# New instruction orders in a sparse attention, longer tile lists for two expert layers, and chains at stage ends spread over engines

## The chip, the cores and the metric

The kernel runs on one core of a Trainium2 chip. The metric is the device time of one execution in microseconds (us).

## The reference

A block of four layers with residuals over x of 16 x 256 tokens with 128 channels, all float32. `norm` is a layer norm.

```python
x = x + linear_attention(norm(x))     # 4 heads; softmax over k's tokens; its own norm and residual inside
x = x + ffn(norm(x))
x = x + sparse_attention(norm(x))
x = x + ffn(norm(x))                  # the same weights

def ffn(x):                           # 8 experts, 128 -> 512 -> 128
    probs = softmax(x @ Wr + br)
    e, gate = argmax(probs), max(probs)
    return (relu(x @ W1[e] + b1[e]) @ W2[e] + b2[e]) * gate

def sparse_attention(x):              # each of 256 queries of a batch keeps 32 keys
    Q, K, V = split(x @ w_qkv.T + b_qkv); Q, K = rope(Q), rope(K)
    iq, ik, iw = ...                  # 4 index heads of 64, one weight for each head
    scores = sum_h relu(iq[h] @ ik.T) * iw[h]
    bias = 0 at the 32 largest scores of a row, -inf elsewhere
    return softmax(Q @ K.T / sqrt(128) + bias) @ V @ w_o.T + b_o
```

## The kernel before

Tokens lie in 32 tiles of 128 (two tiles make one batch, `b`). Each engine has its own list of instructions, written out by hand; they meet in semaphores. The stages follow each other:

1. **Linear attention** (`steps` over 16 batches, a software pipeline: `st.item(k)` is the batch that entered k steps ago). Its end turns the normalised rows (`turn_xf` on TensorE, `xf_out` on ScalarE), multiplies by the router (`router`) and copies the logits (`logits_out`), batch by batch, in `bank[6]`.
2. **Routing 0.** `route_differences`, `route_exp`, `route_choices` and `route_gates` are done for tiles 0 to 23 (k = 0) and 24 to 31 (k = 1). Then ranks, the places of all tokens in the order by expert (`is_tile`, `oneh_slot`, and 32 matmuls at L600), the lists `te` (expert) and `ti` (tile) of the 39 pieces of work and the gather indices `gidx`. `keep_clock` on TensorE issues transposes whose result nobody reads.
3. **Experts 0.** GpSimd gathers sorted rows from DRAM (L427). Step s on TensorE: turn tile s (L620), first layer of piece s-1 (L629), second layer of piece s-2 (L639). ScalarE copies the turned tile (L836) and the expert's first weights (L841) and makes half of `hT` (L849), VectorE the other half (L1184), then `gm` (L1176), `yb` (L1190) and the sum into `big` (L1196). The entries of `te` and `ti` are read into registers by `loaded` (L297), eight at a time, on TensorE, ScalarE and VectorE. TensorE moves on when both halves of `hT` are there.
4. **Sparse attention.** Rows come back by a gather of `X` (L447, `gather_x`). One step s works on several batches at once: projections, index scores and head sums of batch s, the selection of the 32 largest of batch s-1 (four rounds of MAX8, L1335, and MATCH_REPLACE8, L1338), softmax and PV of batch s-2, the next router's rows of batch s-3. VectorE's list of a step is:

```python
mask_logits(0); add_third(b, r, 1); add_fourth(0); mask_logits(1); add_fourth(1)
for i in range(4):
    MAX8 and MATCH_REPLACE8 for both halves
    # i == 0: xf_b (L1267), shifts (nb, L1242)
    # i == 2: attended (L1250, L1255), spread_x2 (L1215)
    # i == 3: add_third(next, r, 0) (L1279), spread_x3 (L1222), aggregate_both (mv, L1234)
```

GpSimd's list of a step is: cosine product (L481), sine product (L483), their sum `qr` (L487), `add_heads` for both halves (`head_sum`, L466), `inverse_std` (`vpe`, L458, and the power `rs`, L460), `X + bo` (L493), and two gathers (L447). The third-head addition needs `head_sum`, `inverse_std` needs `mv`, `nb` needs `rs`, and ScalarE's next `xb` (L866) needs `nb`. ScalarE copies the index weights `iw` from PSUM (L922); their bias comes by a matmul with one row (L713).

5. **Routing 1** and **experts 1**: as 2 and 3, with a scatter of each finished tile to the output (L433) among the gathers of GpSimd: at step s it issues gather s+8 and then scatter s-8.

The functions that the change touches:

## Time and profile before

| | us |
|---|---|
| median of 3 runs | 523.01 (522.72 to 523.64) |
| the profiled execution | 523.16 |
| its span, first to last instruction | 521.3 |
| busy TensorE, VectorE, ScalarE, GpSimd | 437.5, 377.2, 337.8, 290.4 |
| a step of the sparse attention | 11.40 |
| from a piece to the next in the expert stages | 1.90 |

Linear attention takes the first 84 us, routing 0 up to 110, experts 0 up to 193, the sparse attention up to about 405, routing 1 up to 428, experts 1 to the end. No engine is busy all the time, and each stage has another limit, so the shares of the whole span say little: the page is read by stage, with the timeline of one step, and at each idle stretch with the instruction that ended it (in brackets behind `<-`). "issue" is time in which an engine waited for nothing that the profile shows. The granted clock of TensorE is given as a share of 2.4 GHz, so 0.50 is 1.2 GHz.

### The profile page before, as it was taken

The page shows a single profiled execution, that of the slowest core. Times are in us where ns is not written, and L with a number is a line of the kernel's source. Part 1 is how long each engine was busy: PE and PEld are TensorE (multiplying, and loading weights), DVE is VectorE, ACT ScalarE, POOL GpSimd, SP SyncE. Part 2 cuts the span into 40 slices and gives each one's busy share as a digit, 9 for nine tenths or more (in the row PEclk, how much of TensorE's full clock was granted, in tenths as well). Part 3 has the DMA queues.
Part 4 walks back from the last instruction along what each step waited for, and adds up shares of the span by engine and source line. Part 5 has one row for each costly group of instructions (what it writes and reads, how often), then busy time and mean ns, then how long its engine had stood idle before and what let it go on. Part 6 is the DMA issues. An engine that isn't in the chain of part 4 may idle for free. (4 is left out here: it accounts for less than half of the span.)

```text
span 521.3 us, 11629 instructions
## 1 busy us (share of the span) xinstructions
PE 437.5 (84%) x3048; PEld 383.1 (73%) x3048; DVE 377.2 (72%) x1501; ACT 337.8 (65%) x934; POOL 290.4 (56%) x329
## 2 busy tenths in 40 slices
PE   2689995799999896999988999998876599999981
PEld 1579894788988885667767777776655599988981
DVE  4789984836666651389999999999997656666661
...
GB/s 228 289 163 79 65 82 82 1 73 110 110 90 43 34 37 32 4 17 32 31 31 32 32 45 48 31 32 31 21 21 42 22 27 107 78 77 79 67 42 20
DMA packets 45070, 32.42 MB, mean 62 GB/s; under 512 B 13524, under 2 KB 39508, under 8 KB 45012
## 3 DMA queue, kind: packets, MB, share of 16 engines
...
## 5 line engine op out<-in xcount | busy, mean ns | idle before, releaser
L427 POOL DMA_INDIRECT big<-rows,gidx x64 | 61.6, 963 | 56.7 <-DVE gidx L1152 28.3
L639 PE MATMUL bank<-WE,hT 128*128 x624 | 83.6, 277 | 7.5 <-ACT hT L849 6.0
L629 PE MATMUL bank<-X,w 128*128 x624 | 83.4, 277 | 1.2 <-ACT X L836 0.4
L639 PEld LDWEIGHTS bank<-WE,hT 128*128 128x128 f32 x624 | 75.9, 192 | 9.6 <-issue 9.5
L629 PEld LDWEIGHTS bank<-X,w 128*128 128x128 f32 x624 | 75.8, 192 | 3.2 <-issue 3.1
L668 PE MATMUL bank<-xbT,WB 128*128 128x256 f32 x224 | 60.2, 400 | 9.3 <-ACT iq L890 8.7
L1184 DVE TENSOR_SCALAR hT<-bank,w 128x128 f32<-128x128 f32 x156 | 47.5, 346 | 22.7 <-PE bank L629 11.3
L841 ACT ACTIVATE w<-WE 128x644 f32 x78 | 57.2, 734 | 3.9 <-DVE big L1196 3.4
L447 POOL DMA_INDIRECT X<-x,pidx x32 | 31.7, 990 | 47.4 <-DMA x<-big 39.9
L836 ACT ACTIVATE X<-bank 128x128 f32<-128x128 f32 x64 | 17.8, 278 | 59.1 <-PE bank L620 58.9
L668 PEld LDWEIGHTS bank<-xbT,WB 128*128 128x128 f32 x224 | 40.1, 195 | 20.3 <-ACT iq L890 14.8
L849 ACT ACTIVATE hT<-bank,w 128x128 f32<-128x128 f32 x156 | 48.4, 365 | 9.5 <-PE bank L629 9.5
L1338 DVE MATCH_REPLACE8 wk<-m,wk 128x256 f32<-128x256 f32 x128 | 51.2, 407 | 0.0
L1335 DVE MAX8 m<-wk 128x8 f32<-128x256 f32 x128 | 47.4, 411 | 0.0
L433 POOL DMA_INDIRECT out<-big,gidx x32 | 31.4, 982 | 15.7 <-DVE big L1196 9.6
L687 PE MATMUL bank<-ik,iq 64*128 64x256 f32 x256 | 39.0, 403 | 0.8 <-ACT big L932 0.7
L1196 DVE SCALAR_TENSOR_TENSOR big<-yb,gm,big 128x128 f32 x78 | 27.6, 354 | 16.0 <-DVE yb L1190 14.2
L932 ACT ACTIVATE big<-bank 128x512 f32<-128x512 f32 x64 | 34.7, 596 | 2.5 <-PE bank L687 1.5
L1190 DVE TENSOR_TENSOR yb<-bank,w 128x128 f32<-128x128 f32 x78 | 22.6, 290 | 13.7 <-PE bank L639 13.3
L1279 DVE SCALAR_TENSOR_TENSOR wk<-big,iw,head_sum 128x256 f32<-128x256 f32 x32 | 21.1, 660 | 14.8 <-POOL head_sum L466 14.8
L937 ACT ACTIVATE big<-big,iw 128x256 f32<-128x256 f32 x64 | 29.0, 500 | 1.0
L514 PE MATMUL bank<-cst 128*128 128x128 f32 x188 | 28.4, 325 | 0.9 <-DVE big L1196 0.9
...
## 6 DMA issues: line engine op xcount, KB each, us to landing
...
big<-rows,gidx POOLq DMA_INDIRECT x64, 2.8
...
```

The source lines that it names most:

```text
L427: pool.indirect_dma_start(xg[:, j, :], None, rows_dram[n], bass.IndirectOffsetOnAxis(ap=gidx[:, j:j + 1], axis=0)).then_inc(f["g"][j % G_R ...
L447: pool.indirect_dma_start(X[:, t, :], None, x2_dram, bass.IndirectOffsetOnAxis(ap=pidx[:, t:t + 1], axis=0)).then_inc(b_["x"][r], 16)
L629: mm = pe.matmul(bank[r + 2 * (k // 2)][:, k % 2 * P:(k % 2 + 1) * P], w1[st.slot(1, 4)][:, k * P:(k + 1) * P], moving, start=True, stop=True)
L639: mm = pe.matmul(bank[4 + r][:, 0:D], hT[r][:, k, :], WE[:, bass.ds(expert[(s - 2) % TURN], 1), W2_AT + k * D:W2_AT + (k + 1) * D].rearran ...
L668: mm = pe.matmul(to, WB[:, i * D:(i + 1) * D], xbT[r][:, :], start=True, stop=True)
L687: mm = pe.matmul(bank[h % 2][:, h // 2 * S:(h // 2 + 1) * S], iq[r][lo:lo + IDX_DIM, h // 2, c * P:(c + 1) * P], ik[r][lo:lo + IDX_DIM, :] ...
L841: act.activation(w1[st.slot(0, 4)][:, :], WE[:, bass.ds(expert[st.base], 1), 0:W1_LEN].rearrange("p a w -> p (a w)"), ACT.Copy).then_inc(f ...
L849: act.activation(hT[r][:, k, :], bank[r][:, k * P:(k + 1) * P], ACT.Relu, bias=w1[st.slot(1, 4)][:, B1_AT + k:B1_AT + k + 1]).then_inc(f[" ...
L932: act.activation(rel[r][:, c, i::2, :], bank[i][:, :].rearrange("p (h k) -> p h k", h=2), ACT.Relu).then_inc(b_["rel"], 1)
L1184: dve.tensor_scalar(hT[r][:, k, :], bank[2 + r][:, k % 2 * P:(k % 2 + 1) * P], w1[st.slot(1, 4)][:, B1_AT + k:B1_AT + k + 1], 0.0, ALU.add ...
L1335: dve.max(m8[:, c, :], wk[r][:, c, :]).then_inc(b_["v"], 1)
L1338: dve.match_replace(wk[r][:, c, :], m8[:, c, :], wk[r][:, c, :], NEG).then_inc(b_["v"], 1)
```

## The change

- **Sparse attention, VectorE:** both masks first, then both third and both fourth additions, all at the head of a step; the first third addition no longer stands at the end of the step before. `index_weights`, the addition of the index bias, is a VectorE instruction after the second round; the copy on ScalarE and the matmul with one row go away. `nb` of batch 0 is made before the statistics of batch 1.
- **Sparse attention, GpSimd:** the first head sum goes ahead of `qr`, and the gathers ahead of `X + bo`.
- **TensorE there:** the turn of the probabilities of the first half goes behind the last projection.
- **Tile lists:** ScalarE and VectorE load 32 entries at once, then the remaining 7; TensorE loads 32 tiles and 20 experts before its first step, 19 experts at step 22 and 7 tiles at step 33.
- **Ends of stages:** the last three batches of the first stage turn in two banks alternately, with the turn of one ahead of the router of the one before. `route_differences`, `route_exp`, `route_choices` and `route_gates` of the first 24 tiles move to other places in both stages' ends. The number of `keep_clock` transposes changes, and there are new ones.

```diff
+LIST, EXPERTS = 32, 20
...
-KEEP_ROUTE, KEEP_GATHER = 32, 60
+KEEP_SLOTS, KEEP_ROUTE, KEEP_RANK, KEEP_GATHER, KEEP_STATS = 22, 28, 8, 44, 14
...
+        def late(b):
+
+            return bank[2] if isinstance(b, int) and b >= B - 3 and b % 2 else bank[6]
...
-            for c in range(C):
-                sp.dma_start(rowc[:, c * IDX_HEADS:(c + 1) * IDX_HEADS], b_iw).then_inc(ld_w, 16)
+            sp.dma_start(biw_bc[:, :], b_iw.rearrange("a e -> (a e)").partition_broadcast(P)).then_inc(ld_w, 16)
...
                                        ALU.mult).then_inc(b_["rp"], 1)
+                    add_heads(b, r, 0)
                     pool.wait_ge(b_["rp"], 2 * (b + 1))
                     after(pool, b_["S"], C * (b - 1))
                     pool.tensor_tensor(qr[r][:, :, :], qk[r][:, 0:2, :], qk[r][:, 2:4, :], ALU.add).then_inc(b_["qr"], 1)
-                    add_heads(b, r, 0)
                     add_heads(b, r, 1)
                 inverse_std(s)
+                if b + 3 < B:
+                    gather_x(b + 3)
                 if b < B:
                     pool.wait_ge(b_["xb"], b + 1)
                     pool.tensor_tensor(X[:, b * C:(b + 1) * C, :], X[:, b * C:(b + 1) * C, :],
                                        bo_bc[:, :].unsqueeze(1).to_broadcast([P, C, D]), ALU.add).then_inc(b_["xo"], 1)
-                if b + 3 < B:
-                    gather_x(b + 3)
...
-            def turn_xf(n, b, r, where):
+            def turn_xf(n, b, r, where, spare=0):
...
-                after(pe, t["xfT"], b)
-                after(pe, t["lg"], b)
+                after(pe, t["xfT"], b - spare)
+                after(pe, t["lg"], b - spare)
...
                 if st.base == 6:
-                    pe.wait_ge(ld_w, 80)
+                    pe.wait_ge(ld_w, 64)
+                if st.base >= B + 2:
+                    if st.on(5, B):
+                        keep_clock(3, bank[1][:, 0:P])
+                        turn_xf(0, st.item(5), st.slot(5, 2), late(st.item(5)), 1)
                 if st.on(6, B):
-                    router(0, st.item(6), st.slot(6, 2), bank[6][:, S:S + C * E])
+                    router(0, st.item(6), st.slot(6, 2), late(st.item(6))[:, S:S + C * E],
+                           int(st.base >= B + 4))
...
-                if st.on(5, B):
+                if st.on(5, B) and st.base < B + 2:
...
+                keep_clock(KEEP_RANK, bank[1][:, 0:P])
                 pe.wait_ge(rt["rank"], n + 1)
...
-                keep_clock(KEEP_ROUTE, bank[2][:, 0:P])
+                keep_clock(KEEP_SLOTS, bank[2][:, 0:P])
...
-                    if s % TURN == 1 and st.on(1, NT):
-                        tile = loaded(mybir.EngineType.PE, ti, s - 1, TURN, T - 1)
-                    if s % TURN == 2 and st.on(2, NT):
-                        expert = loaded(mybir.EngineType.PE, te, s - 2, TURN, E - 1)
+                    if s == 0:
+                        tile = loaded(mybir.EngineType.PE, ti, 0, LIST, T - 1)
+                        expert = loaded(mybir.EngineType.PE, te, 0, EXPERTS, E - 1)
+                    if s - 1 == LIST:
+                        tile = loaded(mybir.EngineType.PE, ti, LIST, NT - LIST, T - 1)
+                    if s - 2 == EXPERTS:
+                        expert = loaded(mybir.EngineType.PE, te, EXPERTS, NT - EXPERTS, E - 1)
...
-                        moving = xgT[:, bass.ds(tile[(s - 1) % TURN], 1), :].rearrange("p a d -> p (a d)")
+                        moving = xgT[:, bass.ds(tile[(s - 1) % LIST], 1), :].rearrange("p a d -> p (a d)")
...
-                                           WE[:, bass.ds(expert[(s - 2) % TURN], 1), W2_AT + k * D:W2_AT + (k + 1) * D
+                                           WE[:, bass.ds(expert[(s - 2) % EXPERTS], 1), W2_AT + k * D:W2_AT + (k + 1) * D
...
             keep_clock(KEEP_GATHER, bank[4][:, 0:P])
+            pe.wait_ge(b_["x"][0], 16 * C)
+            keep_clock(KEEP_STATS, bank[4][:, 0:P])
...
+                if st.base == B + 1:
+                    keep_clock(10, bank[2][:, 0:P])
...
                     b, r = st.item(2), st.slot(2, 2)
                     after(pe, b_["prT"], b)
-                    turn_probabilities(b, r, 0)
                 if st.on(0, B):
                     project(3)
                 if st.on(2, B):
+                    turn_probabilities(b, r, 0)
                     turn_probabilities(b, r, 1).then_inc(b_["PT"], 1)
...
-                    pe.matmul(bank[5][:, S:S + C * IDX_HEADS], ones[0:1, :], rowc[:, 0:C * IDX_HEADS], start=True, stop=False)
...
-                                       WB[:, 9 * D:9 * D + IDX_HEADS], start=False, stop=(c == C - 1))
+                                       WB[:, 9 * D:9 * D + IDX_HEADS], start=True, stop=True)
...
+                if st.base == B + 1:
+                    keep_clock(2, bank[2][:, 0:P])
...
+                if st.base == B + 2:
+                    keep_clock(8, bank[2][:, 0:P])
...
+                if st.on(5, B) and st.base >= B + 2:
+                    xf_out(0, st.item(5), st.slot(5, 2), late(st.item(5))[:, 0:S])
                 if st.on(6, B):
-                    logits_out(0, st.item(6), bank[6][:, S:S + C * E])
+                    logits_out(0, st.item(6), late(st.item(6))[:, S:S + C * E])
+                if st.base == B + 2:
+                    route_exp(0, 0)
...
-                if st.on(5, B):
+                if st.on(5, B) and st.base < B + 2:
...
-                    if opens(st, 0) and st.on(0, NT):
-                        expert = {}
-                        count = HEAD if st.base == 0 else NT - T if st.base == T else TURN
-                        for k, v in enumerate(loaded(mybir.EngineType.Activation, te, s, count, E - 1)):
-                            expert[st.base + k] = v
+                    if s % LIST == 0 and st.on(0, NT):
+                        expert = loaded(mybir.EngineType.Activation, te, s, min(LIST, NT - s), E - 1)
...
-            route_exp(0, 0)
...
+                if st.base == B + 1:
+                    route_exp(1, 0)
...
-                if st.on(0, B):
-                    act.wait_ge(b_["pj"], 5 * (b + 1))
-                    after(act, b_["wk"], C * (b - 1))
-                    act.activation(iw[r][:, :, :],
-                                   bank[5][:, S:S + C * IDX_HEADS].rearrange("p (c h) -> p c h", c=C),
-                                   ACT.Copy).then_inc(b_["iwe"], 1)
                 for c in range(C):
...
                             after(act, b_["hs"], C * (b - 1))
-                            act.wait_ge(b_["iwe"], b + 1)
                         for i in range(2):
...
                         act.wait_ge(b_["rel"], 2 * (C * b + c + 1))
+                        act.wait_ge(b_["iwe"], b + 1)
                         for h in range(2):
...
-                if st.base == B + 1:
-                    route_exp(1, 0)
...
+                if st.base == B + 1:
+                    dve.wait_ge(ld_wb, 48)
+                    dve.wait_ge(rt["exp0"], 1)
+                    route_differences(0, 0)
...
-                    if opens(st, 2) and st.on(2, NT):
-                        tile = {}
-                        count = HEAD - 2 if st.base == 2 else 9 if st.base == T else TURN
-                        for k, val in enumerate(loaded(mybir.EngineType.DVE, ti, s - 2, count, T - 1)):
-                            tile[st.base - 2 + k] = val
+                    if (s - 2) % LIST == 0 and st.on(2, NT):
+                        tile = loaded(mybir.EngineType.DVE, ti, s - 2, min(LIST, NT - (s - 2)), T - 1)
...
-                        at = bass.ds(tile[st.base - 2], 1)
+                        at = bass.ds(tile[(s - 2) % LIST], 1)
...
-            dve.wait_ge(ld_wb, 48)
-            dve.wait_ge(rt["exp0"], 1)
-            route_differences(0, 0)
...
+
+            def index_weights(b, r):
+
+                dve.wait_ge(b_["pj"], 5 * (b + 1))
+                dve.tensor_tensor(iw[r][:, :, :], bank[5][:, S:S + C * IDX_HEADS].rearrange("p (c h) -> p c h", c=C),
+                                  biw_bc[:, :].unsqueeze(1).to_broadcast([P, C, IDX_HEADS]), ALU.add).then_inc(b_["iwe"], 1)
...
-            shifts(Step(0), 0)
+                if u == -2:
+                    shifts(Step(0), 0)
...
-                if st.on(1, B):
-                    b, r = st.item(1), st.slot(1, 2)
                 if st.on(2, B):
                     p, q = st.item(2), st.slot(2, 2)
                     mask_logits(0)
+                    mask_logits(1)
                 if st.on(1, B):
+                    b, r = st.item(1), st.slot(1, 2)
+                    after(dve, b_["pen"], C * (b - 1))
+                    add_third(b, r, 0)
                     add_third(b, r, 1)
                     add_fourth(0)
-                if st.on(2, B):
-                    mask_logits(1)
-                if st.on(1, B):
                     add_fourth(1)

                 def beside(i):

+                    if i == 1 and st.on(0, B):
+                        index_weights(st.item(0), st.slot(0, 2))
                     if i == 0 and st.on(3, B):
                         xf_b(st)
+                    if i == 0 and st.base == B + 1:
+                        route_differences(1, 0)
                     if i == 0 and st.on(-1, B):
                         shifts(st, -1)
...
-                    if i == 3 and st.on(0, B):
-                        after(dve, b_["pen"], C * (st.item(0) - 1))
-                        add_third(st.item(0), st.slot(0, 2), 0)
...
-                if st.base == B:
-                    route_differences(1, 0)
                 if st.base == B + 1:
                     route_choices(1, 0)
+                if st.base == B + 2:
                     route_gates(1, 0)
```

## Rows read from the trace of the kernel before

**Rows 1.** Busy time of three stretches (stretch, us, busy and count by engine, clock, DMA)
```profile
206.00:208.00 2.00, 2.00 (x6) 1.61 (x5) 0.28 (x2) 0.84 (x2) 0.00 (x0) 0.51 0.00 0
284.58:295.98 11.40, 10.45 (x66) 8.24 (x65) 10.95 (x47) 10.62 (x30) 9.49 (x10) 1.00 0.14 35
448.80:497.00 48.20, 45.15 (x392) 43.89 (x391) 29.79 (x113) 33.12 (x93) 36.90 (x38) 1.00 0.25 73
```

**Rows 2.** Timeline of VectorE over the turn of a step (start us, us, what)
```profile
305.56 0.92 DVE L1279 SCALAR_TENSOR_TENSOR wk<-big,iw,head_sum 128x256 f32<-128x256 f32 x1 [0.28 <-POOL head_sum L466]
306.40 0.48 DVE L1222 BATCH_NORM_STATS2 stat<-X 128x6 f32<-128x128 f32 x2
...
308.02 0.48 DVE L1285 SCALAR_TENSOR_TENSOR wk<-big,iw,wk 128x256 f32<-128x256 f32 x1
...
310.60 0.59 DVE L1267 TENSOR_SCALAR xf<-X,mv,rs 128x128 f32<-128x128 f32 x2
311.11 0.15 DVE L1242 SCALAR_TENSOR_TENSOR nb<-mv,rs 128x2 f32<-128x2 f32 x1
```

**Rows 3.** Timeline of GpSimd in the same step
```profile
307.47 0.20 POOL L458 TENSOR_TENSOR vpe<-mv,eps 128x4 f32<-128x4 f32 x1 [1.27 <-DVE mv L1234]
307.75 1.26 POOL L460 TENSOR_TENSOR rs<-vpe,mhalf 128x4 f32<-128x4 f32 x1
309.00 0.82 POOL L493 TENSOR_TENSOR X<-X,bo_bc 128x256 f32<-128x256 f32 x1
309.99 1.04 POOL L447 DMA_INDIRECT X<-x,pidx  x1 [0.17 <-issue]
311.33 0.95 POOL L447 DMA_INDIRECT X<-x,pidx  x1 [0.30 <-issue]
```

**Rows 4.** Timeline of VectorE and GpSimd at 368 us
```profile
367.99 1.54 DVE L1267 TENSOR_SCALAR xf<-X,mv,rs 128x128 f32<-128x128 f32 x2
...
368.10 1.34 POOL L481 TENSOR_TENSOR big<-big,cst 128x512 f32<-128x512 f32 x1 [0.89 <-ACT big L890]
...
369.45 1.24 DVE L1242 SCALAR_TENSOR_TENSOR nb<-mv,rs 128x2 f32<-128x2 f32 x1
```

**Rows 5.** The line of the first power (durations min/median/max, start, forms)
```profile
L382 POOL TENSOR_TENSOR r<-v,mhalf x5: 1045/2900/2911, 7.2 to 31.9; 128x16 f32<-128x16 f32 x3, 128x4 f32<-128x4 f32 x1, 128x12 f32<-128x12 f32 x1
```

**Rows 6.** Timeline of TensorE at two of the eight holes
```profile
126.20 1.06 PE L629 MATMUL bank<-X,w 128*128 x8
...
129.56 1.15 PE L629 MATMUL bank<-X,w 128*128 x8
...
494.70 1.06 PE L629 MATMUL bank<-X,w 128*128 x8
...
498.52 1.15 PE L629 MATMUL bank<-X,w 128*128 x8 [0.23 <-DVE hT L1184]
```

**Rows 7.** The line that loads registers (ns min/median/max, first and last start)
```profile
L297 ACTq TENSOR_LOAD <-te x10: 543/548/985, 103.9 to 491.9; - x10
L297 PEldq TENSOR_LOAD <-ti x10: 587/594/778, 109.7 to 493.5; - x10
L297 DVEq TENSOR_LOAD <-ti x10: 810/1870/2306, 112.9 to 493.6; - x10
```

**Rows 8.** Timeline at the end of the first stage
```profile
89.16 0.18 ACT L758 ACTIVATE logits<-bank 128x16 f32<-128x16 f32 x1 [1.11 <-PE bank L508]
...
91.88 0.16 DVE L1035 TENSOR_TENSOR r_a<-logits,br_bc 128x64 f32<-128x64 f32 x1
```

**Rows 9.** Timeline at the start of the sparse attention
```profile
203.17 0.88 ACT L866 ACTIVATE xb<-X,nb,rs 128x128 f32<-128x128 f32 x2 [11.39 <-DVE nb L1242]
```

**Rows 10.** Timelines of VectorE and TensorE at the second routing
```profile
398.49 0.42 DVE L1293 CUSTOM_DVE_ANT_0 lg<-bank,pen 128x256 f32<-128x256 f32 x1
...
420.02 4.11 PE L600 MATMUL bank<-oneh_tile,oneh_slot 128*128 128x64 bf16 x32
```

**Rows 11.** Timeline of the last scatter
```profile
511.94 0.97 POOL L433 DMA_INDIRECT out<-big,gidx  x1 [0.30 <-DVE big L1196]
```

18 lines of the change are left out of this document (9 added, 9 removed).

## Prediction

> **What bounds the kernel now.** I read the page first, then the profile by stage. In the middle of the sparse attention one step (one batch of 256 tokens) takes 11.40 us, VectorE is busy 10.95 of it, ScalarE 10.62, TensorE 10.45, and each of the other engines could do with less [rows 1]. So the question is who waits for whom. The timeline of VectorE shows it: at 305.56 the first third-head addition (L1279) starts late, behind GpSimd's `head_sum`, and then takes 0.92 us, where its twin L1285 takes 0.48 [rows 2]. GpSimd in turn waits for `mv` before it starts the inverse deviation [rows 3]. That is a ring: aggregate, GpSimd's whole list of a step, head sum, addition, statistics, aggregate. The wait before the addition is 0.35 us and the addition holds VectorE 0.84 us (305.56 to 306.40), so L1279 at this place costs 1.19 us a step.
>
> Why 0.92? GpSimd ran the second head sum. The clearest case is at 368: `xf` takes 1.54 us for two tiles (0.59 otherwise) and `nb` 1.24 us (0.15 otherwise), each until GpSimd's tensor-tensor of that moment ends (L481 from 368.10 to 369.44, then L483) [rows 2, 4]. VectorE instructions with two SBUF inputs, and `xf`, thus wait for a GpSimd tensor-tensor that began before them. Whoever is first wins, and the order of both lists decides it.
>
> The expert stages are bound by TensorE at 1.90 us a tile, except once every eight tiles: from 126.20 to 129.56 is 3.36 us, and from 494.70 to 498.52 it is 3.82 [rows 6]. There are eight such holes; together they take 13.0 us more than normal tiles (1.90, and 1.79 where no row is turned any more). What they share is the load of the next list entries into registers: 0.55 us on ScalarE, 0.59 on TensorE, but a median of 1.87 on VectorE [rows 7], and TensorE then waits for `hT`. The ends of the stages (clock 0.5, engines mostly waiting) are serial chains.
>
> **Ends of the first stage, routing 0.** Before, the last logits land at 89.34, and only then come the exponential, `choices` and `gates` of the first 24 tiles; the second part begins at 91.88, 2.54 us later [rows 8]. In the new order these are done while TensorE still works on the last batches, so the second part follows the logits directly: -2.5. The turns of the last three batches now overlap in two banks: the last logits come some 1.1 us earlier at the low clock (the three extra transposes a step eat part of it). `KEEP_SLOTS` of 22 lets the slot matmuls start when the slots are ready, about 0.4 earlier here. Together -4.0, bounds -2.5 (no overlap won) and -5.5 (full clock).
>
> **Experts 0.** The four holes vanish: -6.6 of the 13.0. What comes back: VectorE loads 7 entries at step 34 (1.0 taken, between 0.2 and 1.7), TensorE reloads 19 experts and 7 tiles (0.5 together), and at the start TensorE loads 32 + 20 entries in front of its first transpose. The cost of a long load is not in the trace. Bounds: the time doesn't depend on the count (eight entries 0.55, seven 0.985 on ScalarE, so it is not proportional [rows 7]), or it grows with the count: 52 x 0.59/8 = 3.8 us on TensorE, 32 x 1.87/8 = 7.5 us on VectorE. I take about 1.2 us for 32 and 1.0 for 20, one small step for each further eight. Before, the first loads were partly hidden behind the keep-clock transposes and gathers; I charge 0.7. VectorE's first load of 32 stands at step 2, where the second `hT` has some 1 us of slack: free at 1.5 us, dear at 7.5. Sum -6.6 + 1.5 + 0.7 = -4.4.
>
> The Trainium skill speaks against this part: "Runtime: NRT & Kernel Launch", Instruction fetch mechanics, gives about 200 ns a register for such a load even in bulk. By it eight registers would take 1.6 us, and the row for ScalarE says 0.55, so the trace does not agree. By the page's figure, as an estimate, 52 registers would hold TensorE 10.4 us in each expert stage, and the sum would end near 522.
>
> **Start of the sparse attention.** `nb` of batch 0 stood behind the statistics of batch 1, which waited for their gather; ScalarE idled 11.39 us until 203.17 [rows 9]. Now it follows the inverse deviation, at 201.8: -1.2. TensorE gets 14 more transposes after the first gather, so its gap shrinks from 4.0 to 1.6 us; the granted clock, 0.51 from 206 to 208 [rows 1], may hold: I take -0.8 of a possible -1.7. Sum -2.0.
>
> **A step of the sparse attention.** Time zero is the end of the aggregate (307.39). VectorE before: first mask at -0.08, `xf` at 3.21, `nb` at 3.72 [rows 2]. The change puts both masks first, then both thirds and both fourths: one more addition ahead, so `xf` goes to 3.61, its second tile to 3.86, `nb` to 4.12. Taken out of the end of the step: 1.19. Added: 0.40 for the addition without wait, 0.17 for `index_weights` (an addition of 128x8 from PSUM). Step: 11.40 - 1.19 + 0.57 = 10.78.
>
> Now GpSimd. Before: `vpe` at 0.08, power at 0.36 for 1.26, `X + bo` at 1.61, gathers at 2.60 and 3.94 [rows 3]. The power alone takes 1.05 (the 128x4 form of L382 [rows 5]); the 0.21 more is L1279 at 0.23. In the new order a mask stands there, from PSUM, and doesn't block: power ends at 1.41. Then the gathers: the first starts into a fourth (1.37 to about 1.72), then 1.03 + 0.31 + 0.95, ending at 4.01. So `X + bo` asks at about 4.03, in the middle of the second tile of `xf` (3.86 to 4.04) and before `nb` (4.12). It wins against `nb`, which waits until 4.75: +0.50. The step becomes 11.28, 0.12 less than before; 12 steps give -1.4. Without that clash 10.78, -7.4. This is the finest reading of the whole sum: 0.2 us either way changes its sign.
>
> ScalarE loses L922 and the 0.53 us before the second exponential; it could do 10.5. TensorE loses L713. Neither sets the step. The wait for `iwe` now falls on VectorE's second round (5.8), when TensorE wants to turn `xf` (5.5 to 5.8); queued behind it are the scores of the second half and S, with over 0.5 us of slack: nothing.
>
> **The rest.** `route_differences(1, 0)` stood before the last masks (at 398.49, 0.95 late [rows 10]) and now hides in the 3.4 us wait for PV: -0.95. The last `xf` no longer waits for `gates`: -0.6. The slot matmuls began at 420.02, because 32 transposes at half clock were ahead, with the slots ready at 418.8: -1.25 [rows 10]. Gathers start 2.8 earlier. In experts 1 GpSimd is as full as TensorE: from 448.80 to 497.00 it issues 38 gathers and scatters, 36.9 us busy plus 0.30 between two [rows 1]. Without holes TensorE would gain 6.4 less 1.5, but it has the long loads in front, and then the scatters, issued 1.28 apart, set the end. Following that list, the first scatter comes 1.9 earlier, 15 pairs later it is still packed, and the last scatter (511.94 [rows 11]) falls at about 506.9: -5.0 for all of this paragraph.
>
> **Sum.** -4.0 - 4.4 - 2.0 - 1.4 - 5.0 = -16.8. The profiled execution took 523.16 us (span 521.3), the median of the runs is 523.01; so 523.0 - 16.8 = 506.2. I say 506. Its own range is 501 to 511.
>
> **Rivals.**
> 1. *No clash of `nb`* (20%). If `X + bo` asks 0.2 us later, `nb` passes and a step is 10.78: 506 - 6 = 500. For it: rows of single instructions jitter by 0.02 only, but the sum of five durations is not that sure.
> 2. *A double clash* (18%). If `X + bo` asks before 3.95, it beats the second tile of `xf`, and then the cosine product beats `nb`, as at 368 [rows 4]. `nb` ends at 5.87: a step of 12.4, +13 instead of -1.4: 520. Against it: 0.08 us.
> 3. *Long loads are dear* (12%). With the proportional cost TensorE loses 1.6 and VectorE some 4 more in each stage: 506 + 11 = 517.
> 4. *Slower than before* (5%). VectorE's load: six entries took 0.81, eight 1.87 [rows 7], a slope of 0.53 an entry. If that holds, 32 entries take 14.6 us in front of the second `hT`, and every engine stands: +12.6 in each stage, 506 + 25 = 531. It decides from a load of about 10 us on; below that the kernel is still faster.
> 5. *GpSimd's power blocks too*. The Trainium skill, "SBUF — State Buffer", SBUF: two separate sides, says that whoever starts first holds the pair for the whole instruction. The power from 0.36 to 1.41 would then hold up the third at 0.57 for 0.84 us a step, 10 us in all, 516. Rows speak against it: L1285 ran at 0.63 (308.02) in 0.48 us inside a power of 1.26 [rows 2, 3], so I give it 3%.
> 6. *The change does nothing measurable* (2%): gains in the stages given back in the sparse attention, 523.
>
> My forecast has the remaining 40%. From 498 to 521 leaves out no more than 2 in 10: below it only a case in which clock and clash both turn out well, above it dear loads or two bad cases at once. Faster by more than 0.2% (about what a measurement of this kernel can tell): 0.92; within: 0.02; slower: 0.06.
>
> **What would show it.** A step between aggregates of 11.3 us, with `nb` (the shift before the second round) at 0.7 instead of 0.15 us; 0.15 says rival 1, 1.7 with a long `xf` says rival 2. No wait of VectorE for `head_sum`. Third additions at 0.48. No hole at every eighth tile, one each near step 22 and 34. The duration of the register load with 32 entries: about 1.2 to 1.5 us is my case, above 4 rival 3. The second part of routing 0 starts right behind the last logits. Scatters packed until the end. I am wrong if loads of 32 take long, or if `X + bo` arrives elsewhere than at 4.0.

## The result, and the profile after

The changed kernel takes 530.24 us (median of 10 runs, 528.25 to 533.32), the kernel before, beside it, 522.77 us: a ratio of 1.013, 95% interval 1.0104 to 1.0157. It is slower by a little over 1%. (Ratios here and below are the recorded ones; the quotient of two medians differs from them by up to 0.002.) The prediction was 506 us, with 498 to 521 as range and 6% for slower. One of the four executions of run 10 below, the profiled one, fell in a slower state of the chip (547.88 us), so its time and ratio go by the other three, and of its trace only the steps of the sparse attention are read.

The profiled execution of the changed kernel took 528.76 us, its span is 526.9 (521.3 before), and the mean granted clock of TensorE is 0.916 (0.938 before). First, where the time went, by landmarks that both kernels have: the indices of the gathers (`gidx`), the first gather of `X` in the sparse attention, the first MAX8, the last aggregate, and the last scatter.

| stretch | before | after | difference | in the sum |
|---|---|---|---|---|
| start to `gidx` of routing 0 | 105.39 | 98.51 | -6.9 | -4.0 |
| to the first gather of `X` (experts 0) | 90.61 | 87.24 | -3.4 | -4.4 |
| to the first MAX8 (start of the sparse attention) | 22.77 | 19.51 | -3.3 | -2.0 |
| to the last aggregate (sparse attention) | 186.20 | 208.75 | +22.6 | -1.4, and its tail some -1.5 |
| to `gidx` of routing 1 | 19.45 | 17.86 | -1.6 | with experts 1 some -3.5 |
| to the last scatter (experts 1) | 87.52 | 85.66 | -1.9 | (see above) |
| to the end | 9.37 | 9.37 | 0 | 0 |

So every stretch around the sparse attention gained, 17.0 us together, and the sparse attention lost 22.6. The lines with the first and last starts of these landmarks, of the kernel after (the three numbers after the count are ns, minimum, median and maximum):

```profile
L1170 DVE CAST gidx<-idxf x2: 181/182/183, 98.5 to 431.9; 128x32 uint32<-128x32 f32 x2
L451 POOL DMA_INDIRECT X<-x,pidx x32: 938/959/1183, 185.8 to 362.0; - x32
L1354 DVE MAX8 m<-wk x128: 401/409/424, 205.3 to 405.6; 128x8 f32<-128x256 f32 x128
L1246 DVE BATCH_NORM_AGGREGATE mv<-stat x64: 146/150/183, 190.1 to 414.0; 128x2 f32<-128x6 f32 x64
L1285 DVE TENSOR_SCALAR xf<-X,mv,rs x32: 332/633/3191, 226.4 to 415.7; 128x128 f32<-128x128 f32 x32
```

The last line is the find. `xf` took 10.3 us in all before (32 tiles of 0.34 us median, one of them 1.29); now it is 37.2 us, a median of 0.63 and up to 3.19 for one tile. Busy time of two steps of the kernel after, measured between the ends of two aggregates (columns as in [rows 1]), stands against the one step of 11.40 there:

```profile
289.26:304.08 14.82, 11.80 (x60) 8.72 (x58) 13.82 (x48) 10.90 (x31) 9.13 (x10) 0.80 0.10 28
304.08:316.72 12.64, 12.60 (x68) 10.35 (x69) 11.47 (x48) 9.96 (x28) 9.20 (x10) 0.83 0.11 31
```

From the third batch's aggregate on the steps, taken between the starts of the aggregates, are 12.98, 10.82, 13.79, 13.81, 11.82, 14.45, 12.63, 14.82, 12.64, 14.82, 13.81, 12.61, 14.82 us. The one of 10.82 is the last in which VectorE has no `xf` to do yet; the trouble starts with the first `xf`. VectorE in the step of 14.82 us (start us, us, what), the answer to [rows 2]:

```profile
293.87 3.74 DVE L1285 TENSOR_SCALAR xf<-X,mv,rs 128x128 f32<-128x128 f32 x2
297.53 0.15 DVE L1254 SCALAR_TENSOR_TENSOR nb<-mv,rs 128x2 f32<-128x2 f32 x1
```

And GpSimd beside it, the answer to [rows 3]:

```profile
293.33 0.96 POOL L451 DMA_INDIRECT X<-x,pidx  x1 [0.30 <-issue]
294.32 0.76 POOL L499 TENSOR_TENSOR X<-X,bo_bc 128x256 f32<-128x256 f32 x1
295.05 1.26 POOL L485 TENSOR_TENSOR big<-big,cst 128x512 f32<-128x512 f32 x1
296.27 1.25 POOL L487 TENSOR_TENSOR big<-big,cst 128x512 f32<-128x512 f32 x1
```

The reader is to see that `xf` ends when the sine product ends (297.52): its second tile got nothing while `X + bo`, the cosine product (L485) and the sine product (L487) ran one behind the other. `nb` was never held, it was only late. The two tiles by themselves:

```profile
L1285 DVE TENSOR_SCALAR xf<-X,mv,rs x2: 630/1910/3191, 293.9 to 294.4; 128x128 f32<-128x128 f32 x2
```

The first took 0.63 us where 0.33 is usual, and so the second, which starts 0.25 us after the first where nothing is in the way, started at 294.42, 0.10 after `X + bo` (294.32). In the shorter steps (xf at 308.22, 1.29 us for two tiles) the cosine product had to wait for ScalarE, and only `X + bo` came between.

What follows from the late `nb`, on ScalarE and TensorE in the same step:

```profile
297.72 0.88 ACT L886 ACTIVATE xb<-X,nb,rs 128x128 f32<-128x128 f32 x2 [2.91 <-DVE nb L1254]
```
```profile
298.65 0.69 PE L671 MATMUL bank<-cst,xb 128*128 128x128 f32 x2 [2.48 <-ACT xb L886]
```

TensorE stands for 2.5 us in such a step, and its granted clock in three stretches of 25 us is 0.86, 0.84 and 0.80 (1.00 before in the stretches beside them), so part of the next step runs at the lower of the two levels (1.2 instead of 2.4 GHz; 341.00 to 343.00 shows 0.50):

```profile
230.00:255.00 25.00, 20.02 (x98) 15.54 (x99) 24.69 (x95) 18.77 (x50) 15.93 (x19) 0.86 0.11 30
280.00:305.00 25.00, 21.98 (x119) 17.11 (x119) 22.84 (x88) 20.02 (x54) 16.19 (x18) 0.84 0.12 33
330.00:355.00 25.00, 21.31 (x108) 16.47 (x106) 23.70 (x89) 17.94 (x50) 16.45 (x18) 0.80 0.12 32
```

The loads of the tile lists, whose price the prediction had to guess (beside [rows 7]): four on each engine and list, two of the full 32 (TensorE's experts 20) and two of the rest.

```profile
L302 DVEq TENSOR_LOAD <-ti x4: 1065/1596/2364, 106.8 to 504.5; - x4
L302 ACTq TENSOR_LOAD <-te x4: 974/1482/2159, 97.3 to 498.7; - x4
L302 PEldq TENSOR_LOAD <-ti x4: 1070/1634/2322, 100.2 to 500.4; - x4
L302 PEldq TENSOR_LOAD <-te x4: 1362/1612/1925, 102.5 to 477.3; - x4
```

### The profile page after: what moved, and what is told of

Its sections match the earlier page's. It is cut to its first block, busy times and chain, and to the rows that moved or that the text cites. A ratio compares the mean times of both kernels' runs of the same rounds, so it can differ in the third digit from the quotient of the medians.

```text
span 526.9 us, 11585 instructions
## 1 busy us (share of the span) xinstructions
PE 443.9 (84%) x3031; PEld 388.9 (74%) x3031; DVE 401.1 (76%) x1517; ACT 333.5 (63%) x918; POOL 286.3 (54%) x329
## 4 chain that ended last, share of the span: by engine, by line
PE 39%; DVE 19%; issue 14%; POOL 9%; ACT 9%; DMA 1%; POOLq 0%; ACTq 0%; DVEq 0%; SPq 0%
PE bank L642 12%; PE bank L652 12%; DVE xf L1285 5%; PE bank L683 3%; DVE wk L1357 3%; DVE m L1354 3%; PE bank L518 2%; ACT big L947 2%; PE bank L702 2%; PE bank L610 2%; DVE wk L1304 2%; PE bank L761 2%; PE bank L633 1%; DVE wk L1298 1%; POOL X L451 1%
## 5 line engine op out<-in xcount | busy, mean ns | idle before, releaser
L683 PE MATMUL bank<-xbT,WB 128*128 128x256 f32 x224 | 63.9, 432 | 7.2 <-ACT iq L910 6.4
L683 PEld LDWEIGHTS bank<-xbT,WB 128*128 128x128 f32 x224 | 45.7, 216 | 20.6 <-ACT iq L910 11.3
L470 POOL TENSOR_TENSOR head_sum<-big 128x256 f32<-128x256 f32 x32 | 23.3, 727 | 41.6 <-ACT big L953 41.6
L702 PE MATMUL bank<-ik,iq 64*128 64x256 f32 x256 | 41.1, 431 | 0.1
L1211 DVE SCALAR_TENSOR_TENSOR big<-yb,gm,big 128x128 f32 x78 | 27.6, 354 | 16.0 <-DVE yb L1205 15.4
L1285 DVE TENSOR_SCALAR xf<-X,mv,rs 128x128 f32<-128x128 f32 x32 | 37.2, 1202 | 0.5 <-POOL rs L464 0.5
L886 ACT ACTIVATE xb<-X,nb,rs 128x128 f32<-128x128 f32 x32 | 14.2, 500 | 34.1 <-DVE nb L1254 34.0
L518 PE MATMUL bank<-cst 128*128 128x128 f32 x203 | 33.5, 333 | 2.5 <-DMA X<-x,pidx 1.5
## 6 DMA issues: line engine op xcount, KB each, us to landing
WE<-b SPq DMA_DIRECT2D x1, 512.0 KB, 11.5
```

The source lines that it names most:

```text
L683: mm = pe.matmul(to, WB[:, i * D:(i + 1) * D], xbT[r][:, :], start=True, stop=True)
L702: mm = pe.matmul(bank[h % 2][:, h // 2 * S:(h // 2 + 1) * S], iq[r][lo:lo + IDX_DIM, h // 2, c * P:(c + 1) * P], ik[r][lo:lo + IDX_DIM, :] ...
L1285: ins = dve.tensor_scalar(xf[r][:, c, :], one_tile(b, c), mv2[u][:, C + c, 0:1], rs2[u][:, C + c:C + c + 1], ALU.subtract, ALU.mult)
```

## The experiments

Five theories were set against each other. **P**: the chain at SBUF is the loss (GpSimd's instructions hold `xf`; without that a step is about 10.8 us). **N**: the late `nb`, with ScalarE and TensorE behind it, is the loss. **R**: the new order of the third additions is. Then, for what keeps VectorE out: **Q**: GpSimd's next tensor instruction does, while the gather in front of it still runs; **G**: the gather itself does.

The runs were made on three chips. The kernel before took 561.73 us on that of runs 1 to 4, 522.47 on that of 5 to 8 and 562.51 on that of 9 to 12 (more on this at the end), so only ratios to the kernel before on the same chip are compared, and steps between aggregates, which agree between chips to some hundredths of a us. Each ratio is given with its 95% interval. The kernel after stands at 1.013, beside a kernel before of 522.77 us; on the two slower chips it was not run, so a ratio of runs 1 to 4 or 9 to 12 is not compared with its 1.013 but their sparse attention with its own (the table at the end of this section).

**1. `X + bo` before the gathers again, the rest as after.**

```diff
                 inverse_std(s)
-                if b + 3 < B:
-                    gather_x(b + 3)
                 if b < B:
                     pool.wait_ge(b_["xb"], b + 1)
                     pool.tensor_tensor(X[:, ...], ..., ALU.add).then_inc(b_["xo"], 1)
+                if b + 3 < B:
+                    gather_x(b + 3)
```

> The kernel after, with one thing undone: GpSimd adds the bias to X before it issues the two gathers of a step, as before. Theory P (the chain at SBUF: the gather and X + bo hold xf until the cosine and sine products are ready too): xf falls from 1.29 or 3.74 us to 0.59, nb comes on time, a step falls from 12.6 to 14.8 us to about 10.8, which is what the step without xf at 211.56 took (10.82). 13 steps times about 2.7 us: 530 - 35 = 495 us. Theory R (the loss is in the third additions, which now wait at the head of a step for GpSimd's second head sum and ScalarE's penalties, and xf only fills a wait that would be there anyway): steps stay at 12.5 or more, 522 to 530 us.

Measured: 570.42 us, ratio 1.0139 [1.0064, 1.0214]. Theory P's time did not come. But its trace doesn't speak for R either: each of the first eleven `xf` takes 3.3 to 3.4 us or 0.59 and nothing between, and the steps with 0.59 are the shorter ones (11.7 to 12.7 us), but for one of 14.1, in which `nb` was held for 2.85 us. The gathers now end at the place where `X + bo` ended, and behind them stands the cosine product. At 303.69:

```profile
303.69 0.95 POOL L451 DMA_INDIRECT X<-x,pidx  x1 [0.30 <-issue]
304.67 1.27 POOL L485 TENSOR_TENSOR big<-big,cst 128x512 f32<-128x512 f32 x1
305.90 1.26 POOL L487 TENSOR_TENSOR big<-big,cst 128x512 f32<-128x512 f32 x1
```
```profile
304.23 3.28 DVE L1285 TENSOR_SCALAR xf<-X,mv,rs 128x128 f32<-128x128 f32 x2
```

`xf` began 0.44 us before the cosine product and was held all the same. 14 us later, in the same run, it passes (0.33 us a tile) beside the same gather, and there the cosine product had to wait for ScalarE:

```profile
318.46 0.95 POOL L451 DMA_INDIRECT X<-x,pidx  x1 [0.30 <-issue]
320.01 1.28 POOL L485 TENSOR_TENSOR big<-big,cst 128x512 f32<-128x512 f32 x1 [0.61 <-ACT big L910]
```
```profile
L1285 DVE TENSOR_SCALAR xf<-X,mv,rs x2: 330/332/334, 318.6 to 318.8; 128x128 f32<-128x128 f32 x2
```

This is where theory Q came from. The step in which `nb` was held shows the same within one gather (the first line is the last of the seven copies that the cosine product waits for):

```profile
344.46 0.49 ACT L910 ACTIVATE big<-bank,COL 128x256 f32<-128x256 f32 x1
344.56 0.96 POOL L451 DMA_INDIRECT X<-x,pidx  x1 [0.30 <-issue]
345.54 1.27 POOL L485 TENSOR_TENSOR big<-big,cst 128x512 f32<-128x512 f32 x1
```
```profile
344.70 0.59 DVE L1285 TENSOR_SCALAR xf<-X,mv,rs 128x128 f32<-128x128 f32 x2
345.20 2.85 DVE L1254 SCALAR_TENSOR_TENSOR nb<-mv,rs 128x2 f32<-128x2 f32 x1
```

The cosine product had its data at 344.95. The second tile of `xf`, started at that moment (0.39 us into the gather), passed; `nb`, started 0.25 us later, was held until the sine product ended (348.02). In the step at 236.56 the data had been there since 235.68, and a second tile at the same place in the gather (0.38 us) took 3.18 us.

**2. `nb` before `xf`, the rest as after.**

```diff
-                    if i == 0 and st.on(3, B):
-                        xf_b(st)
                     ...
                     if i == 0 and st.on(-1, B):
                         shifts(st, -1)
+                    if i == 0 and st.on(3, B):
+                        xf_b(st)
```

> The kernel after, with VectorE's nb (the shift that ScalarE needs for the next normalised rows) put before xf instead of behind it. Theory N (what costs is that nb is late: ScalarE starts the normalised rows 3 us late, TensorE waits and its clock falls): nb takes 0.15 us at its place, ScalarE and TensorE keep step, about 510 us. Theory P (VectorE's own time in the long xf is what costs): xf is still overtaken, and since ScalarE is then early, the cosine and sine products are ready in every step, so xf takes 3.7 us each time and a step is 10.8 + 3.15 = about 14 us: 530 to 535 us.

Measured: 568.02 us, ratio 1.0103 [1.0043, 1.0164]. `nb` takes 0.57 us and is in time, yet the steps are as long as without this edit (12.4 to 15.0 us), with `xf` at 3.5 or 1.0 us. N falls as the main cause: what VectorE loses inside `xf` is lost whether or not ScalarE gets `nb` in time. P's forecast of a 3.7 us `xf` in every step was too high; in about every third step the cosine product was still late.

**3. `X + bo` on one element a partition.**

```diff
-                    pool.tensor_tensor(X[:, b * C:(b + 1) * C, :], ..., bo_bc[:, :]..., ALU.add)
+                    pool.tensor_tensor(X[:, b * C:b * C + 1, 0:1], ..., bo_bc[:, 0:1]..., ALU.add)
```

> The kernel after, with X + bo done on one element a partition instead of 256 (this leaves the bias of the attention's output out of nearly all of X; its time at the same place is then about 0.2 us instead of 0.76). If the gather is what holds xf's first tile, that tile still takes 0.63 us; if it was X + bo, 0.33. Theory P: the second tile comes to run, but the cosine product asks about 0.7 us after xf began, so that it can beat nb where it is ready: nb of 0.15 in some steps and over 1 us in others, 500 to 520 us. Theory R: as the kernel after, 528 to 532.

This leaves the bias of the attention's output out of nearly all of `X`; only times are read from it. Measured: 564.48 us, ratio 1.0048 [1.0015, 1.0081]. `xf` takes 3.4 or 3.2 us in each of its first eleven steps, which are 13.4 to 13.9 us long. The first tile is now held from the start in every other step, through `X + bo` (0.20 us), the cosine and the sine product. So a short `X + bo` doesn't let `xf` through; a product is ready behind it in every one of these steps. The question of the expectation (gather or `X + bo`) could not be read from it.

**4. GpSimd's new order of gathers alone, in the kernel before.**

```diff
+                if b + 3 < B:
+                    gather_x(b + 3)
                 if b < B:
                     pool.wait_ge(b_["xb"], b + 1)
                     ...
-                if b + 3 < B:
-                    gather_x(b + 3)
```

> The kernel before, with GpSimd's new order of the gathers alone (both before X + bo); VectorE keeps its old order, so xf is asked for 3.2 us after the aggregate and nb at 3.7, and X + bo at about 4.2. Theory P: no overtaking, since both are through before X + bo asks; at most the gather holds xf's first tile for 0.3 us: 522 to 527 us. If GpSimd's order by itself is the harm (whatever VectorE does): 530 or more.

Measured: 585.06 us, ratio 1.0425 [1.0351, 1.05], the slowest of all. Theory P's branch of the expectation (522 to 527 us) was too low by some 20 us on the chip that it was reckoned for, and the other branch (the order itself is the harm) came true:

```profile
320.58 0.96 POOL L447 DMA_INDIRECT X<-x,pidx  x1 [0.30 <-issue]
321.57 0.76 POOL L495 TENSOR_TENSOR X<-X,bo_bc 128x256 f32<-128x256 f32 x1
322.29 1.25 POOL L481 TENSOR_TENSOR big<-big,cst 128x512 f32<-128x512 f32 x1
323.51 1.26 POOL L483 TENSOR_TENSOR big<-big,cst 128x512 f32<-128x512 f32 x1
```
```profile
320.64 1.10 DVE L1267 TENSOR_SCALAR xf<-X,mv,rs 128x128 f32<-128x128 f32 x2
321.67 3.12 DVE L1242 SCALAR_TENSOR_TENSOR nb<-mv,rs 128x2 f32<-128x2 f32 x1
```

`xf` runs entirely beside the gather, and `X + bo` starts only at 321.57; still its second tile, started at 320.89, took 0.85 us, and then `nb`, two elements a partition, waited 3 us for three GpSimd instructions. A step with such an `nb` is 14.1 to 14.8 us long, one in which the cosine product came late (`nb` 0.68) 11.6 to 13.0. The new order of the gathers is harmful by itself; the new order on VectorE isn't what makes it so.

**5. `X + bo` waits for `nb`, one step too early.**

```diff
                     pool.wait_ge(b_["xb"], b + 1)
+                    pool.wait_ge(b_["nb"], min(b + 2, B))
```

> The kernel after, with one wait more: GpSimd starts X + bo of a step only when VectorE has made nb of that step. No other order changes. Theory Q (what takes the port is GpSimd's next tensor instruction, once its data are there, while the gather in front of it still runs; a gather with nothing ready behind it holds nothing): now nothing is ready behind the second gather, xf takes 0.59 us, nb 0.15, and a step falls to about 10.8 us: 0.94 to 0.95 of the time before. Theory G (the second half of a gather holds VectorE's xf by itself): xf still takes 0.3 to 0.5 us more, nothing longer, a step of 11.2 to 11.4: 0.95 to 0.965. Theory R (the loss is in the new order of the third additions): no gain over the kernel after, 1.01.

Measured: 530.25 us, ratio 1.0141 [1.0084, 1.0198]. GpSimd's step s meets step s + 1 of VectorE, so the `nb` waited for had long been made, and the wait held nothing. Steps and times are those of the kernel after (most steps 12.5 to 14.8 us); the run says nothing on Q or G, and was made again as run 9.

**6. `xf` and `nb` before the first MAX8, the rest as after.**

```diff
+                if st.on(3, B):
+                    xf_b(st)
+                if st.on(-1, B):
+                    shifts(st, -1)
                 rounds = TOP_K // 8
                 for i in range(rounds):
                     ...
-                    if i == 0 and st.on(3, B):
-                        xf_b(st)
-                    if i == 0 and st.on(-1, B):
-                        shifts(st, -1)
```

> The kernel after, with VectorE's xf and nb put before the first MAX8 of a step instead of behind the first round. They then run about 2.3 to 3.0 us after the aggregate, beside GpSimd's first gather, which is followed by another gather and not by a tensor instruction. Theory Q: xf 0.59, nb 0.15, a step of about 10.8 us, 0.94 to 0.95 of the time before. Theory G: the first gather delays xf by 0.3 to 0.5 us: 0.95 to 0.965. Theory R: no gain, about 1.01.

Measured: 494.30 us, ratio 0.9453 [0.9405, 0.9501]: 28 us less than the kernel before. The step is 10.67 us, the clock 1.00:

```profile
298.43:309.10 10.67, 9.89 (x62) 7.89 (x62) 10.50 (x49) 10.44 (x30) 9.19 (x10) 1.00 0.17 40
```
```profile
L1285 DVE TENSOR_SCALAR xf<-X,mv,rs x32: 333/342/368, 225.6 to 381.0; 128x128 f32<-128x128 f32 x32
```

Two instructions were moved by one round, 1.45 us. They now run beside the first gather (300.03 to 301.20), behind which comes another gather. This is the fastest version of the study, 36 us below the kernel after on chips that give the kernel before the same time. R falls: the additions are where the change put them.

**7. The tile lists alone, in the kernel before.**

```diff
+                    if s == 0:
+                        tile = loaded(mybir.EngineType.PE, ti, 0, LIST, T - 1)
+                        expert = loaded(mybir.EngineType.PE, te, 0, EXPERTS, E - 1)
...
+                    if s % LIST == 0 and st.on(0, NT):
+                        expert = loaded(mybir.EngineType.Activation, te, s, min(LIST, NT - s), E - 1)
...
+                    if (s - 2) % LIST == 0 and st.on(2, NT):
+                        tile = loaded(mybir.EngineType.DVE, ti, s - 2, min(LIST, NT - (s - 2)), T - 1)
```

> The kernel before, with the tile lists loaded 32 (TensorE's experts 20) at once and nothing else. By the sum on record: four holes less in each expert stage, the reloads and the longer first load back: -4.4 us in experts 0, and some -3 to -4 in experts 1, where the scatters set the end: -8 us together, 0.985 of the time before. If long loads were dear, 1.00 or more.

Measured: 521.98 us, ratio 0.9991 [0.996, 1.0022]: no change. From `gidx` to the first gather of `X` it is 87.6 us (90.6 before), from the second `gidx` to the last scatter 86.9 (87.5): 3.7 us together. The sparse attention, whose code is that of the kernel before, takes 190.9 us instead of 186.2 and gives it all back, in three steps of 13.98, 12.53 and 14.21 us. `xf` of the first:

```profile
L1265 DVE TENSOR_SCALAR xf<-X,mv,rs x2: 329/1748/3167, 272.8 to 273.0; 128x128 f32<-128x128 f32 x2
```

The second gather started at 272.62 there, 0.39 before the second tile (273.01), and the cosine product was ready. Before, `xf` met the first gather ([rows 2, 3]) and passed. In [rows 2, 3] the second gather begins 0.73 us after `xf`; here it begins 0.14 us before it. So the kernel before stands less than 1 us from the same fall, and an edit in another stage is enough to push some of its steps over.

The same trace shows the other side too: between the held steps four steps of the unchanged code take 10.95 to 10.97 us and not 11.40. In them GpSimd's second head sum starts 0.8 us behind VectorE's addition (317.18 and 316.36), which then takes 0.48 us, where in the kernel before the two meet in every step and it takes 0.92. So 0.44 of the 11.40 us are that meeting.

**8. The ends of the stages alone, in the kernel before** (first stage, routing 0, start of the sparse attention; lists and sparse attention as before).

```diff
+                if st.base >= B + 2:
+                    if st.on(5, B):
+                        keep_clock(3, bank[1][:, 0:P])
+                        turn_xf(0, st.item(5), st.slot(5, 2), late(st.item(5)), 1)
...
+                if st.base == B + 1:
+                    route_differences(0, 0)
...
-            shifts(Step(0), 0)
+                if u == -2:
+                    shifts(Step(0), 0)
```

> The kernel before, with the change's new chains at the ends of the first stage, of routing 0 and at the start of the sparse attention alone (route_differences, route_exp and the turns of the last three batches moved up, fewer keep-clock transposes before the slots, nb of batch 0 earlier); the sparse attention itself and the lists as before. By the sum on record -4.0 and -2.0 us: 0.989. The traces of before and after say more: the indices of the gathers are there 6.9 us earlier, so 0.984.

Measured: 515.69 us, ratio 0.9852 [0.9796, 0.9907], as expected from the two traces: this part is worth 7 us. Beside the trace of the kernel before, 5.1 us are gained up to `gidx`, 0.5 in experts 0, 2.7 at the start of the sparse attention and 1.4 behind it, and the sparse attention itself, whose code is the old one, takes 2.8 more (188.98).

**9. `X + bo` waits for the `nb` of the same time.**

```diff
                     pool.wait_ge(b_["xb"], b + 1)
+                    pool.wait_ge(b_["nb"], min(b + 3, B))
```

> The kernel after, with X + bo waiting for the nb that VectorE makes in the same 11 us (in the run before this one the wait was for the nb one step earlier, which had long been made, so nothing changed). Theory Q (GpSimd's next tensor instruction takes the port while the gather in front of it still runs, if its data are there): nothing is ready behind the second gather, xf takes 0.59 us from 1.29 or 3.74, nb 0.15, a step about 10.8: 0.945 to 0.95 of the time before. Theory G (the gather itself holds xf): xf's first tile stays at 0.63, a step of 11.1 or more: 0.955 to 0.965. Theory R: no gain, 1.01.

Measured: 532.89 us beside 562.51, ratio 0.9493 [0.9461, 0.9526]. Steps of 10.67 us, as Q said, from one wait more and no other order:

```profile
309.73 0.95 POOL L451 DMA_INDIRECT X<-x,pidx  x1 [0.30 <-issue]
311.08 0.72 POOL L500 TENSOR_TENSOR X<-X,bo_bc 128x256 f32<-128x256 f32 x1 [0.40 <-issue]
```
```profile
310.27 0.59 DVE L1286 TENSOR_SCALAR xf<-X,mv,rs 128x128 f32<-128x128 f32 x2
```

`xf` starts 0.54 us into the second gather, exactly as in the kernel after, and its two tiles take their usual 0.59 us together. G falls as the cause. (A small effect is left: the first tile takes 0.46 us instead of 0.34 and ends with the gather, as it does beside the first gather in the kernel before; the second isn't delayed by it.) (Lines behind the added one have numbers one higher here and in run 10.)

**10. The cosine product waits for `nb`, `X + bo` as after.**

```diff
                     pool.wait_ge(b_["pje"], 8 * b + 7)
+                    pool.wait_ge(b_["nb"], min(b + 2, B))
```

> The kernel after, with the cosine product waiting for nb, and X + bo left as it is. Dose and response for theory Q: X + bo still takes the port from xf's second tile, but the cosine and sine products no longer follow, so xf takes 1.29 us in every step and never 3.74. A step of 10.7 + 0.7 = 11.4 to 11.6: about 504 us, 0.96 to 0.97 of the time before. If steps stay at 12.6 or more, the long xf was not what made them long.

Measured: 543.38 us beside 562.51, ratio 0.9654 [0.9599, 0.971]. Steps of 11.37 to 11.38 us: 10.67 and 0.70 for the longer `xf`, no more and no less.

```profile
315.37 0.95 POOL L451 DMA_INDIRECT X<-x,pidx  x1 [0.30 <-issue]
316.33 0.78 POOL L500 TENSOR_TENSOR X<-X,bo_bc 128x256 f32<-128x256 f32 x1
```
```profile
L1286 DVE TENSOR_SCALAR xf<-X,mv,rs x2: 634/688/743, 315.9 to 316.5; 128x128 f32<-128x128 f32 x2
```

Both tiles pay: the first is held although `X + bo` starts only 0.43 us after it, the second by `X + bo` itself.

**11. Run 6 with the old lists of eight.** The loads are put back as they are in the kernel before (the reverse of run 7's diff).

```diff
-                    if s == 0:
-                        tile = loaded(mybir.EngineType.PE, ti, 0, LIST, T - 1)
+                    if s % TURN == 1 and st.on(1, NT):
+                        tile = loaded(mybir.EngineType.PE, ti, s - 1, TURN, T - 1)
```

> The kernel with xf and nb early (494.3 us), with the tile lists loaded eight at once as in the kernel before. In the kernel before the long lists alone gave nothing (0.999), but the sparse attention behind them lost 4.7 us to two steps of 14 us, so their own worth could not be read. Here no step clashes: if the lists are worth what the expert stages show (3.0 us in experts 0, 0.7 to 1.9 in experts 1), 498 to 499.5 us, 0.953 to 0.956; if they are worth nothing, 0.945.

Measured: 539.66 us beside 562.51, ratio 0.9598 [0.9566, 0.9629], against 0.9453 with the new lists on another chip, and above the expectation (0.953 to 0.956, reckoned for that other chip). Steps of 10.67 or 10.68 in both. On this chip experts 0 takes 101.7 us with the old lists and 95.0 with the new (run 9), so the lists are worth 6.7 us there, where they are worth 2.5 to 3.0 on the chip of runs 5 to 8 (90.1 in run 8, 87.1 to 87.6 in runs 5 to 7). The gain is real, and its size depends on the chip.

**12. `xf` and `nb` before the first MAX8 in the kernel before, nothing else.** The same edit as in run 6, in the old file.

```diff
+                if st.on(3, B):
+                    xf_b(st)
+                if st.on(-1, B):
+                    shifts(st, -1)
                 rounds = TOP_K // 8
```

> The kernel before, with xf and nb put before the first MAX8 of a step, and nothing else. It tells whether the gain of that place belongs to the new orders or to the place alone. In the old order of GpSimd X + bo stands before the gathers and asks 1.6 us after the aggregate, so xf at 2.3 meets it, and the addition that waits for the second head sum (1.19 us a step) is still there. Theory Q: a step of 11.4 to 12.0, 1.00 to 1.015. If the place alone is the gain: 10.8, 0.97 or less.

Measured: 561.11 us beside 562.51, ratio 0.9966 [0.994, 0.9992]. The step stays at 11.40 us, although each `xf` now takes 1.01 us (it meets `X + bo` at its old place): 0.4 us more on VectorE disappears in a wait, as it would if the ring of head sum, addition and aggregate sets the old step. The place alone is worth next to nothing; the new additions, the new order of GpSimd and the place are worth 12.9 us of the sparse attention together (173.3 us from the first MAX8 to the last aggregate in run 6, 186.2 before).

**The sparse attention of all runs.** From the first MAX8 to the last aggregate, and the steps of its middle, between aggregates:

| run | us | steps |
|---|---|---|
| before | 186.20 | 11.40 |
| after | 208.75 | 11.8 to 14.8 |
| 1, `X + bo` before the gathers | 209.87 | 11.7 to 15.4 |
| 2, `nb` before `xf` | 211.64 | 12.4 to 15.0 |
| 3, `X + bo` on one element | 207.56 | 13.4 to 13.9 |
| 4, new order of gathers, old rest | 208.96 | 11.6 to 14.8 |
| 5, a wait that holds nothing | 209.06 | 11.5 to 15.2 |
| 6, `xf` and `nb` early | 173.28 | 10.67 |
| 7, lists alone, old rest | 190.88 | 10.95 to 14.2 |
| 8, ends alone, old rest | 188.98 | 11.40 |
| 9, `X + bo` waits for `nb` | 174.75 | 10.67 |
| 10, cosine product waits for `nb` | 183.79 | 11.37 |
| 11, as 6 with the old lists | 173.09 | 10.67 |
| 12, `xf` and `nb` early, old rest | 183.71 | 11.40 |

## Why the prediction was wrong

**What bounds the kernel** was right: the ring through GpSimd's second head sum. Runs 6 and 9 keep the additions that take it out and avoid the clash, and the step falls to 10.67; the prediction worked out 10.78 "without that clash". Run 12 agrees from the other side.

**Ends of the first stage, routing 0**: right in kind, too small. -6.9 us instead of -4.0. The last logits start at 84.97 instead of 89.16 [rows 8], 4.2 us earlier, where 1.1 was taken. 1.0 of this lies ahead of the changed code: the last aggregate of the first stage comes at 81.29 instead of 82.33, and it lies between 81.3 and 82.5 in runs of either code. The other 3.2 are the mis-sized term, the overlap in two banks "at the low clock": from 80 to 85 us the granted clock is 1.00, where it was 0.67.

**Experts 0**: -3.4 instead of -4.4. A load of 32 entries takes 2.0 to 2.4 us on each engine and one of 7 takes 1.0 to 1.1, where about 1.2 and 1.0 were taken. At the start TensorE's first expert matmul comes 7.0 us after `gidx` instead of 6.2, 0.8 where 0.7 was charged. VectorE's first load of 32, taken as free, is the term that was missing: it runs from 106.82 to 109.18, `hT` comes late, and the next piece follows after 2.70 us instead of 1.90. Near the reloads the distances are 2.97, 2.10 and 2.19, some 1.9 us too long together, where 1.5 was taken. Rivals 3 and 4 fell: VectorE's load of 32 takes 2.4 us and not 7.5 or 14.6. The Trainium skill's 200 ns a register ("Runtime: NRT & Kernel Launch", Instruction fetch mechanics) would be, as an estimate, 6.4 us for 32; the trace does not agree.

**Start of the sparse attention**: -3.3 instead of -2.0. `nb` of batch 0 comes 5.7 us after the first gather instead of 7.0, about the -1.2 of the sum; the clock is the mis-sized term: it stays at 1.00 through this stretch, where [rows 1] show 0.51, so the whole 1.7 came and not 0.8. **Routing 1 and experts 1**: -3.5 together, about as in the sum; the scatters are packed until 512.69, as forecast.

**A step of the sparse attention**: this is the step that failed, in the sentence "So `X + bo` asks at about 4.03, in the middle of the second tile of `xf` (3.86 to 4.04) and before `nb` (4.12). It wins against `nb`". The places were right to within some hundredths: in the first three steps with `xf` it starts 3.60 us after the aggregate and `X + bo` at 4.05 (3.61 and 4.03 by the prediction), and in all eleven `X + bo` starts 0.45 us after `xf`. (By the prediction's own interval 4.03 is the end of the second tile, not its middle.) Wrong was the rule that an instruction asks when it starts. Runs 1, 4, 7, 9 and 10 show what holds in its place: *when a gather runs on GpSimd and the tensor instruction behind it has its data, VectorE's `xf` and `nb` are held if they start late enough in the gather, up to 0.7 us before the reported start of that instruction; when it has not, or when another gather stands behind, they are not held.* The edge lies between 0.14 us into the gather (a tile of run 7 passes) and 0.31 (the tile of run 4 is held). With that, the first tile at +0.54 into the gather loses 0.3 us, the second starts behind `X + bo`, and the chain closes.

The Trainium skill has a rule that fits. "GPSIMD Engine Reference", 2.1 Instruction dispatch, says that a core of GpSimd starts the next instruction as soon as it has done its own share of the one before, and "Perfetto Trace Analysis", DMA Instruction — SWDGE (GPSIMD), that only two of its cores make the descriptors of a DMA. By these the other cores would start on `X + bo` while the gather runs. Runs 9 and 10, which differ from the kernel after in one wait each, agree with it; that this is the cause inside the engine is argued and not shown. It could also be that the start which the trace reports for the instruction behind the gather is late; no run tells the two apart.

The second half of the failure is the price. Rival 2 let `X + bo` and the cosine product win and put a step at 12.4 us. It was read off the meeting at 368 [rows 4], where GpSimd stood idle in front of the cosine product and no gather ran, and there GpSimd does let VectorE in between two ready products: the second tile of `xf`, held by the cosine product, gets through when that ends, and only `nb` waits for the sine product. The kernel after has the same in its twelfth step with `xf`, when the gathers are over:

```profile
376.11 1.27 POOL L485 TENSOR_TENSOR big<-big,cst 128x512 f32<-128x512 f32 x1 [1.22 <-ACT big L910]
377.34 1.26 POOL L487 TENSOR_TENSOR big<-big,cst 128x512 f32<-128x512 f32 x1
```
```profile
L1285 DVE TENSOR_SCALAR xf<-X,mv,rs x2: 526/914/1301, 376.9 to 377.4; 128x128 f32<-128x128 f32 x2
```

The first tile gets through between the two products, the second waits for the sine product alone. Behind a gather it is otherwise. In the kernel after and in runs 1 to 4, what is held there, but for the first one ahead of a full `X + bo`, waits to the end of the last instruction that is ready: the second tile of `xf` in the kernel after for `X + bo`, the cosine and the sine product. It costs 3.15 us a step and not 1.1. Neither the prediction nor the rival had a row of such a meeting with a gather in front. Why VectorE is let in in the one case and not in the other is open. Of the first eleven steps with `xf` seven have it and four have 0.70; the twelfth has 1.2 and the thirteenth 1.7: 7 x 3.15 + 4 x 0.70 + 2.9 = 27.8 us, and the whole `xf` line agrees (37.2 in the kernel after, 9.8 in run 6, 27.4 more). The sparse attention of the kernel after is 35.5 us longer than that of run 6 (208.75 to 173.28). The remaining 8 us are what comes behind a held step: ScalarE and TensorE late, TensorE at the lower level, VectorE waiting for the penalties (0.83 us at 290.10, 0.35 at 304.44). In run 10 nothing is held for long, and a step is 10.67 + 0.70 exactly; in the kernel after the steps with the same 1.29 us `xf` are 12.6 (one 11.8). The comparison says that these 1.3 us come from the held step before; how they divide between clock and waits was not tried.

Theory N, that the late `nb` is the main harm, fell with run 2; theory R with runs 6, 9 and 10, which keep the additions of the change. Rival 5 (the power holds the thirds) fell as well: in run 6 the thirds, at 299.01 and 299.41, run inside the power (298.80 to 299.84) at 0.48 us. One sign of the prediction misled: "0.15 says rival 1". `nb` took 0.15 us in the kernel after, and its steps were up to 14.8 us long, because what was held was the `xf` in front of it.

Still open: why the first one held gets through when `X + bo` at full size stands behind the gather (it ends 1.17 us after the start of the gather, whether it started at 0.54, as in the kernel after, or at 0.31, as in run 4), and is held to the end in every other step when `X + bo` is one element wide (run 3), and in both steps of run 1 in which it starts some 0.5 us into the gather with the cosine product behind.
